# Three blocks a turn in the networks without weights to broadcast, six banks and twelve buffers

## The chip, the core and the metric

The kernel runs on one core of one Trainium2 chip. The metric is the device time of one execution in microseconds (us). Before the change it is 3207.71 us, the median of three runs (3206.38 to 3210.78).

## What is computed

The reference is a small vision tower: 64 sequences of 129 tokens with 64 channels each, kept as h (a tokenizer in front makes them from images). Eight stages follow, each added to h after a layer norm: attention and a network, four times over, of different kinds. What matters here are the networks:

```python
# L0_ffn: 8 experts, hidden width 128, the two best of a gate's scores taken
h = gelu(einsum('td,edh->teh', x, W1) + b1)
y = einsum('teh,ehd->ted', h, W2) + b2
out = einsum('ted,te->td', y, mask)          # mask is 1 for two experts, else 0

# L1_attn: four layers, each with linear attention and then
x = x + gelu(ln(x) @ W1[l] + bf1[l]) @ W2[l] + bf2[l]     # 64 -> 256 -> 64

# L1_ffn: half of each sequence's tokens, times a router weight, 64 -> 256 -> 64
# L3_ffn: 8 experts of width 256 with a capacity, relu, times the gate's probability
```

## The kernel before

All tokens lie in SBUF as one array of 128 partitions by 4128 columns: partitions 0 to 63 are the channels of the first 32 sequences, 64 to 127 those of the other 32 (the two halves, HALVES = 2). Columns are worked in 12 tiles of 344 (TILE, TILES). The stages are phases one behind the other; a phase is a Block, at whose end all engines meet, and the next phase starts when the last one has come.

The function mlp_phase (L642) is one such phase. It serves seven networks: L0's experts (L3894), the four dense networks of L1 (L2570, one a layer), L1's half network (L2713) and L3's experts (L2914). In the last two the result is multiplied by a weight for each token. The weights are spread over the partitions by a matmul of its own (WeightedAddTo.broadcast, L2604) into one of two auxiliary banks, aux_ps, which ScalarE copies out. The other five calls end in AddTo (L845), whose broadcast is None: there nothing writes or reads aux_ps.

The hidden width is cut into blocks of 128: 8 blocks (one for each expert) in L0, 2 in a layer of L1. A step is one block of one tile, so a phase has 12 x blocks steps: 96 in L0, 24 in a layer of L1. For each step and half:

- TensorE raises (raise_hidden, L690): w_up, 64 rows by 128 columns, times the tile's half, into a bank of hid_ps. The two halves sit in different rows of the array. In L0 a second matmul in bf16 (L696) adds -1e30 to the tokens that the expert isn't chosen for. A bank must have been emptied by ScalarE (wait on act_done, k - ring + 1).
- ScalarE (L743) takes the bank through GELU with the bias into a buffer of hid.
- TensorE lowers (lower, L716): w_down, 128 rows by 64 columns, times the buffer, added up in the output bank y_ps of the tile; the two halves go to different columns of the array and different partitions of the bank. In L0 each tile ends with a matmul for the experts' bias (L723).
- VectorE adds the tile's output to h or x (L854, L855), once its last block is lowered. In the last layer of L1, GpSimd also adds that to h (L758).

In the trace each fp32 product of TensorE is two matmul instructions (two passes), and the two halves run side by side. The order on TensorE is written out by hand:

```python
for s in range(0, steps + span, span):
    for k in range(s, min(s + span, steps)):
        raise_hidden(k)
    for k in range(max(s - span, 0), min(s, steps)):
        lower(k)
```

A turn of this loop raises span steps and then lowers the span steps of the turn before. With span = 2 that is four products up (two steps, two halves) and four down. The banks are ring = 4 for the hidden values, 2 for the outputs and 2 auxiliary ones, eight in all, which is the whole of PSUM; the buffers of hid are 8. In L3's experts a DMA brings a row for every mask and VectorE multiplies it in (L792); in L0 no DMA runs in the phase.

Of the kernel before, what the change touches and what calls it, by code (L numbers as in the profile page):

```python
# [78 lines left out]
@contextmanager  # L79
def phase(tower):  # L80
    with ExitStack() as stack:
        ph = Phase(tower, stack)
        yield ph
    for s in ph.used:
        s.base += s.total
        tower.free.append(s)
# [554 lines left out]

def mlp_phase(tower, net, func, x, finish, load, experts=None, sum_into=None, store=None):  # L642

    nc, ring, span = tower.nc, 4, 2
    hidden_ring, row_ring = 8, 6
    with phase(tower) as ph:
        w_up, w_down, b_up = net["up"], net["down"], net["bias"]
        w_extra = net["extra"] if experts else None
        blocks = w_up.shape[1]
        hid_ps = [ph.ps(f"hid{r}") for r in range(ring)]  # L650
        y_ps = [ph.ps(f"y{u}") for u in range(2)]
        aux_ps = [ph.ps(f"aux{u}") for u in range(2)]
        hid = [ph.sb(f"hidden{r}", [P, TILE]) for r in range(hidden_ring)]
        steps = TILES * blocks
        up_done = ph.counts(HALVES * steps)
# [1896 lines left out]
def linear_tower(tower, nc, h, x, column):  # L2552

    with ExitStack() as stack:

        hn = stack.enter_context(nc.sbuf_tensor("lin_hn", [P, COLS], F32))
        v_ends = stack.enter_context(nc.sbuf_tensor("lin_v_ends", [TRIO, TRIOS, TRIO, P], F32))
        with ExitStack() as inner:
            pos = inner.enter_context(nc.sbuf_tensor("lin_pos", [P, 4 * SEQ], F32))
            norm_phase(tower, h, x, 1e-5, pos=pos, loads=[(pos, "L1_pos"), (tower.head_blocks, "L1_blocks")])  # L2560
        for l in range(4):
            with ExitStack() as layer:
                maps = Held(layer, tower, f"lin{l}", [(n, [P, P], f"L1_{n}{l}") for n in ("wq", "wk", "wv", "wo")])
                norm_phase(tower, x, hn, 1e-5, gamma=column(f"L1_g1{l}"), beta=column(f"L1_b1{l}"), loads=maps.loads)
                linear_attention_phase(tower, hn, x, maps, column(f"L1_bo{l}"), v_ends, l == 0)
            with ExitStack() as layer:
                net = network(layer, tower, ("L1", l))
                norm_phase(tower, x, hn, 1e-5, gamma=column(f"L1_g2{l}"), beta=column(f"L1_b2{l}"), loads=net.loads,
                           then=ACT.Gelu)
                mlp_phase(tower, net, ACT.Gelu, hn, AddTo(x, column(f"L1_bf2{l}")), None,  # L2570
                          sum_into=h if l == 3 else None)
# [68 lines left out]
def half_ffn(tower, nc, h, x, column):  # L2640

    with ExitStack() as stack:
# [4 lines left out]
        with phase(tower) as ph:  # L2647
# [12 lines left out]
            with nc.Block() as block:  # L2660
# [31 lines left out]
                def _(dve):  # L2692
# [18 lines left out]
                    assert done[0] == 2 * rounds + 3  # L2711
        finish = WeightedAddTo(tower, h, column("L1f_b2"), tower.spread2, rows)
        mlp_phase(tower, net, ACT.Gelu_apprx_tanh, x, finish, finish.load)  # L2713


# [189 lines left out]
def capacity_ffn(tower, nc, h, x, out):  # L2905
    with ExitStack() as stack:
        rows_t = stack.enter_context(nc.sbuf_tensor("cap_rows", [P, COLS], F32))
        marks16 = stack.enter_context(nc.sbuf_tensor("cap_marks16", [P, COLS], BF16))
        net, gate = network(stack, tower, ("L3", ""), "L3_down_b"), gate_weights(stack, tower, "L3")
        counts = Held(stack, tower, "capacity", [("counting", [P, 2, P], "L3_counting"), ("spread", [P, P], "L3_spread")])  # L2910
        gated_norm_phase(tower, h, x, 1e-5, gate, rows_t, 1, copy16=marks16, offset=0.0, counting=counts["counting"],
                         loads=net.loads + gate.loads + counts.loads, then=ACT.Relu)
        finish = WeightedAddTo(tower, h, 0.0, counts["spread"], rows_t, finite=True)
        mlp_phase(tower, net, ACT.Relu, x, finish, finish.load, Experts(rows_t, 2, marks16=marks16), store=out)  # L2914
# [1094 lines left out]
```

## Time and profile before

| | |
|---|---|
| median of 3 runs | 3207.71 us |
| profiled execution, its own time | 3208.76 us |
| its span, first to last instruction | 3207.0 us |
| TensorE busy in the span | 3012.3 us (94%) |
| L0's experts, from the first raise to the last read | 573.5 to 723.4 us |
| L1's four dense networks | 847.2 to 880.6, 986.6 to 1020, 1124.6 to 1158, 1262.5 to 1297 us |
| granted TensorE clock over the span | 0.99 |

PE is TensorE, PEld its weight loads, ACT ScalarE, DVE VectorE, POOL GpSimd. Times in a view are microseconds from the start of the span. TensorE's matmuls overlap in the pipeline: a matmul of these networks is recorded with 0.45 us, but another starts while it ends, so a row of several matmuls is shorter than their sum, and TensorE can be called busy all through a stretch in which it streams no data for a part of the time.

### The profile page before, as it was taken

What the parts mean: (1) busy time and instruction counts of PE and PEld (TensorE: products, weight loads), DVE (VectorE), ACT (ScalarE), POOL (GpSimd) and SP (SyncE); (2) the same over time, 40 slices, a digit from 0 to 9 for tenths busy, and PEclk for the clock granted to TensorE, in tenths of its full rate; (3) what the DMA queues carried; (4) which work ended last, traced back from release to release, by engine and by line L of the source; (5) the groups of instructions that cost most, each with busy time, mean ns of one, the idle gap of its engine ahead of it and who ended that gap; (6) DMA issues with size and microseconds to landing.
All of it is one profiled execution on the core that took longest, in us unless ns stands there. A gap on an engine that the chain in (4) does not pass through costs nothing. (4 is left out here: it accounts for less than half of the span.)

```text
span 3207.0 us, 61051 instructions
## 1 busy us (share of the span) xinstructions
PE 3012.3 (94%) x22529; PEld 1889.7 (59%) x22561; DVE 2147.3 (67%) x4191; ACT 1736.0 (54%) x3881; POOL 1170.7 (37%) x1151
## 2 busy tenths in 40 slices
PE   7999989999999999999899999997899999989999
PEld 6999867446565655467565543334566666664444
DVE  7999835106474645359669744447999999956777
ACT  1322334566667566657535443344666666665666
POOL 4666611001010101018357323225777777740000
PEclk9999989999999999999999999999999999999999
DMA  2000000000000000000000032210000000004776
GB/s 92 16 16 16 1 19 13 1 1 8 3 5 7 4 5 4 4 7 2 9 1 1 28 76 54 58 43 19 17 7 5 5 5 5 4 25 43 68 67 66
DMA packets 75679, 66.43 MB, mean 21 GB/s; under 512 B 20518, under 2 KB 70857, under 8 KB 74969
## 3 DMA queue, kind: packets, MB, share of 16 engines
q1 hardware_dynamic: 75384, 62.52, 11.6%
q8 instruction: 183, 3.00, 0.4%
q14 instruction: 112, 0.91, 0.1%
HBM read 55.58 MB, written 2.51 MB: 18 GB/s over the span
## 5 line engine op out<-in xcount | busy, mean ns | idle before, releaser
L743 ACT ACTIVATE p_hidden<-p_hid_ps,net_bias 128x344 f32<-128x344 f32 x816 | 382.4, 549 | 225.7 <-PE p_hid_ps L690 167.1
L716 PE MATMUL p_y_ps<-p_hidden,net_down 128*64 128x344 f32 x1632 | 286.0, 467 | 4.6 <-DVE p_hidden L792 4.6
L2875 DVE TENSOR_TENSOR p_hid<-p_silu,p_pair_ps 128x344 f32<-128x344 f32 x288 | 134.8, 509 | 161.5 <-PE p_pair_ps L2824 82.5
L690 PE MATMUL p_hid_ps<-xn,net_up 64*128 64x344 f32 x1248 | 238.0, 481 | 1.2 <-PEq L333 0.6
L792 DVE TENSOR_TENSOR p_hidden<-p_hidden,p_row 128x344 f32<-128x344 f32 x384 | 175.1, 514 | 78.8 <-ACT p_hidden L743 44.1
L2856 ACT ACTIVATE p_silu<-p_pair_ps 128x344 f32<-128x344 f32 x288 | 116.0, 454 | 190.8 <-PE p_pair_ps L2813 190.8
L1983 POOL TENSOR_TENSOR p_prob<-p_prob,p_total 128x1024 f32<-128x1024 f32 (+1 forms) x128 | 185.3, 1469 | 52.5 <-DVE p_total L2171 52.5
L2546 POOL TENSOR_TENSOR p_qt<-p_qt,p_q_sum 97x512 f32<-97x512 f32 (+1 forms) x44 | 46.4, 1054 | 427.3 <-DVE p_q_sum L2489 427.3
L716 PEld LDWEIGHTS p_y_ps<-p_hidden,net_down 128*64 128x64 f32 x1632 | 103.3, 136 | 160.6 <-issue 49.7
L1970 POOL TENSOR_TENSOR p_rot<-p_rot,p_cross 128x512 f32<-128x512 f32 x128 | 160.1, 1273 | 96.4 <-DVE p_cross L2145 96.4
L2802 POOL TENSOR_TENSOR p_weighted<-routed_hn,sent_row 128x344 f32<-128x344 f32 x96 | 89.1, 950 | 241.3 <-PE p_pair_ps L2829 206.3
L690 PEld LDWEIGHTS p_hid_ps<-xn,net_up 64*128 64x128 f32 x1248 | 104.5, 186 | 121.0 <-ACT p_hidden L743 77.4
L1205 POOL TENSOR_TENSOR p_prob<-p_prob,p_total 128x516 f32<-128x516 f32 (+1 forms) x128 | 130.8, 1043 | 66.7 <-DVE p_total L1327 66.7
L154 PE MATMUL p_var_ps<-p_square,average 128*128 128x344 f32 x360 | 139.1, 470 | 2.4 <-DVE p_square L204 1.3
L1824 PE MATMUL p_late_ps<-shared_keys,p_q_t 64*128 64x128 f32 x1024 | 136.7, 287 | 0.0
L1824 PE MATMUL p_early_ps<-shared_keys,p_q_t 64*128 64x64 f32 x1024 | 129.4, 267 | 0.0
L1824 PEld LDWEIGHTS p_early_ps<-shared_keys,p_q_t 64*128 64x128 f32 x1024 | 126.7, 191 | 0.0
L2168 DVE TENSOR_REDUCE p_total<-p_prob 128x8 f32<-128x1024 f32 (+1 forms) x128 | 115.7, 945 | 16.4 <-ACT p_prob L2044 16.4
L3034 PE MATMUL p_c_ps<-p_in,p_crossed 128*128 128x128 f32 (+1 forms) x768 | 126.0, 286 | 0.0
L1824 PEld LDWEIGHTS p_late_ps<-shared_keys,p_q_t 64*128 64x128 f32 x1024 | 124.3, 189 | 0.0
L1977 POOL TENSOR_TENSOR p_rot<-p_rot,p_root 128x1024 f32<-128x1024 f32 x64 | 121.8, 1903 | 0.2
L2037 ACT ACTIVATE p_q_t<-p_t_ps 128x512 f32<-128x512 f32 x128 | 75.9, 594 | 81.3 <-PE p_t_ps L1799 81.3
(487 smaller groups left out, 8045.9 us busy)
## 6 DMA issues: line engine op xcount, KB each, us to landing
sent_row<-gated_rows SPq DMA_DIRECT2D x192, 86.0 KB, 2.9
p_row<-mark_rows SPq DMA_DIRECT2D x192, 86.0 KB, 10.3
tok_x<-in_tok_x SPq DMA_DIRECT2D x11, 384.0 KB, 3.1
out<-h SPq DMA_DIRECT2D x12, 172.0 KB, 3.6
shared_swapped<-xn SPq DMA_DIRECT2D x64, 32.0 KB, 1.9
shared_value_pairs<-shared_values SPq DMA_DIRECT2D x16, 128.0 KB, 2.5
p_x<-in_tok_x SPq DMA_DIRECT2D x5, 384.0 KB, 3.1
p_kinds<-in_tok_c3w SPq DMA_DIRECT2D x1, 1280.0 KB, 7.2
```

Source lines behind the costliest of these rows:

```text
L154: pe.matmul(var_ps[t % var_banks][:, 0:TILE], tower.average[:], square[t % ring][:], start=True, stop=True).then_inc(var_ready.sem, 1)
L690: mm = pe.matmul(hid_ps[k % ring][:, 0:TILE], w_up[half(g), n, :], x[half(g), cols(t)], start=True, stop=not experts or by_rows)
L716: mm = pe.matmul(y_ps[u][half(g), 0:TILE], w_down[:, n, :], hid[k % hidden_ring][:], start=n == 0, stop=last and not experts)
L743: act.activation(hid[k % hidden_ring][:], hid_ps[k % ring][:, 0:TILE], func, bias=b_up[:, n:n + 1]).then_inc(act_done.sem, 1)
L792: dve.tensor_tensor(hid[k % hidden_ring][:], hid[k % hidden_ring][:], row[x % row_ring][:, g, :], ALU.mult).then_inc(masked.sem, 1)
L1205: pool.tensor_tensor(p[:], p[:], total[(j - 1) % 2][:, g, :, None] .to_broadcast([P, HEADS, seen]), ALU.mult).then_inc(scaled.sem, 1)
L1824: return pe.matmul(ps[:, c * wide:(c + 1) * wide], q, keys_t[half(p), b, 0:wide], start=ty == LATE and i == 0, stop=ty == EARLY and i == 3)
L1970: pool.tensor_tensor(a[:, :, s, :], a[:, :, s, :], x[:, :, 1 - s, :], ALU.add).then_inc(added.sem, 1)
L1977: pool.tensor_tensor(r, r, root[n % ring_q][:, :, None].to_broadcast([P, Q_HEADS, D]), ALU.mult).then_inc(normed.sem, 1)
L1983: pool.tensor_tensor(p[:], p[:], total[n % 2][:, ty, :, None].to_broadcast([P, MS, wide]), ALU.mult).then_inc(scaled.sem, 1)
L2875: dve.tensor_tensor(hid[n % ring_h][g][:], silu[n % 2][g][:], c_of(n, g)[:, 0:TILE], ALU.mult).then_inc(hid_ready.sem, 1)
L3034: pe.matmul(sides[:, :, side, :].rearrange("p n (b i) -> p n b i", i=half_rows), weights, shifted(group, y, s), start=False, stop=closes[0 ...
```

## The change

In a call whose finish has no broadcast, a turn raises three steps and lowers three, the hidden banks are six and the hidden buffers twelve. The two auxiliary banks are not allocated there. In a call with a broadcast everything stays: four banks, span 2, eight buffers.

```diff
 def mlp_phase(tower, net, func, x, finish, load, experts=None, sum_into=None, store=None):
 
-    nc, ring, span = tower.nc, 4, 2
-    hidden_ring, row_ring = 8, 6
+    nc = tower.nc
+    ring, span = (4, 2) if finish.broadcast else (6, 3)
+    hidden_ring, row_ring = 2 * ring, 6
...
-        aux_ps = [ph.ps(f"aux{u}") for u in range(2)]
+        aux_ps = [ph.ps(f"aux{u}") for u in range(2)] if finish.broadcast else None
```

## Rows read from the trace of the kernel before

**Rows 1.** The page's first part: engine, busy us, share, instructions.
```profile
PE 3012.3 (94%) x22529; PEld 1889.7 (59%) x22561; DVE 2147.3 (67%) x4191; ACT 1736.0 (54%) x3881; POOL 1170.7 (37%) x1151
```

**Rows 2.** Busy time by stretch: L0, one layer of L1, half network, L3's experts.
```profile
core 0: us, PE busy (x) PEld busy (x) DVE busy (x) ACT busy (x) POOL busy (x), PEclk, DMA share, GB/s
573.50:723.50 150.00, 149.31 (x1008) 67.81 (x1008) 6.20 (x12) 90.71 (x193) 0.00 (x0) 1.00 0.00 1
847.20:880.60 33.40, 32.70 (x192) 14.73 (x192) 6.92 (x12) 23.53 (x49) 0.00 (x0) 1.00 0.00 1
...
1335.00:1378.00 43.00, 42.67 (x214) 16.68 (x216) 11.33 (x21) 28.05 (x61) 0.00 (x0) 1.00 0.00 1
2914.00:3199.00 285.00, 280.36 (x1596) 122.08 (x1596) 206.51 (x482) 184.13 (x396) 0.00 (x0) 0.99 0.71 68
```

**Rows 3.** Waits in 847 to 880: who waited for whom, us, times, longest.
```profile
DVE xn L855 <- PE p_y_ps L716: 26.2, 11, 5.4
ACT p_hidden L743 <- PE p_hid_ps L690: 9.6, 11, 1.3
PEld p_hid_ps L690 <- ACT p_hidden L743: 5.9, 11, 0.6
```

**Rows 4.** TensorE in order of time, 862 to 868 (L1): start, duration, what.
```profile
862.73 1.43 PE L690 MATMUL p_hid_ps<-lin_hn,net_up 64*128 64x344 f32 x8
864.09 1.38 PE L716 MATMUL p_y_ps<-p_hidden,net_down 128*64 128x344 f32 x8
865.39 1.43 PE L690 MATMUL p_hid_ps<-lin_hn,net_up 64*128 64x344 f32 x8
```

**Rows 5.** ScalarE in order of time, 847 to 868 (L1).
```profile
848.07 3.62 ACT L743 ACTIVATE p_hidden<-p_hid_ps,net_bias 128x344 f32<-128x344 f32 x8 [1.15 <-PE p_hid_ps L690]
...
863.61 1.86 ACT L743 ACTIVATE p_hidden<-p_hid_ps,net_bias 128x344 f32<-128x344 f32 x4 [0.80 <-PE p_hid_ps L690]
```

**Rows 6.** TensorE in order of time, first and last turns of a layer of L1.
```profile
847.22 3.61 PE L690 MATMUL p_hid_ps<-lin_hn,net_up 64*128 64x344 f32 x16 [0.40 <-PEq L134]
850.76 1.38 PE L716 MATMUL p_y_ps<-p_hidden,net_down 128*64 128x344 f32 x8
...
876.05 1.43 PE L690 MATMUL p_hid_ps<-lin_hn,net_up 64*128 64x344 f32 x8
877.41 2.53 PE L716 MATMUL p_y_ps<-p_hidden,net_down 128*64 128x344 f32 x16
```

**Rows 7.** TensorE's weight loads in order of time, 862 to 868 (L1).
```profile
862.73 0.88 PEld L690 LDWEIGHTS p_hid_ps<-lin_hn,net_up 64*128 64x128 f32 x8 [0.53 <-ACT p_hidden L743]
864.09 0.78 PEld L716 LDWEIGHTS p_y_ps<-p_hidden,net_down 128*64 128x64 f32 x8 [0.48 <-issue]
```

**Rows 8.** TensorE in order of time, 640 to 643 (a turn of L0).
```profile
640.70 0.85 PE L690 MATMUL p_hid_ps<-xn,net_up 64*128 64x344 f32 x4
641.38 0.31 PE L696 MATMUL p_hid_ps<-unmarked,banish 64*128 64x344 bf16 x2
641.53 0.74 PE L690 MATMUL p_hid_ps<-xn,net_up 64*128 64x344 f32 x4
642.11 0.31 PE L696 MATMUL p_hid_ps<-unmarked,banish 64*128 64x344 bf16 x2
642.35 1.38 PE L716 MATMUL p_y_ps<-p_hidden,net_down 128*64 128x344 f32 x8
```

**Rows 9.** TensorE in order of time, L0's first and last lowerings.
```profile
577.37 1.38 PE L716 MATMUL p_y_ps<-p_hidden,net_down 128*64 128x344 f32 x8
...
719.74 2.53 PE L716 MATMUL p_y_ps<-p_hidden,net_down 128*64 128x344 f32 x16
722.10 0.75 PE L723 MATMUL p_y_ps<-marks,net_extra 128*64 128x344 f32 x4
```

**Rows 10.** VectorE (layer one) and GpSimd (layer four) at the network's end.
```profile
880.02 0.58 DVE L855 SCALAR_TENSOR_TENSOR xn<-p_y_ps,columns,xn 128x344 f32<-128x344 f32 x1 [0.58 <-PE p_y_ps L716]
...
1296.03 0.91 POOL L758 TENSOR_TENSOR h<-h,xn 128x344 f32<-128x344 f32 x1 [0.25 <-DVE xn L855]
```

**Rows 11.** Busy time by stretch, columns as in group 2, behind two attentions.
```profile
828.00:833.00 5.00, 4.88 (x11) 3.02 (x12) 0.14 (x1) 2.13 (x5) 0.00 (x0) 0.66 0.16 40
1104.00:1109.00 5.00, 3.35 (x11) 1.49 (x10) 1.11 (x2) 1.09 (x3) 0.00 (x0) 1.00 0.16 39
```

## The prediction

> **What bounds the kernel now.** I read the page's sums first, to see which engine is full, then the stretches of the five networks that the change touches, then, inside one of them, who waits for whom, and last the order in time of the single turns.
>
> TensorE is busy for 94% of the span [rows 1]. Five networks have no weights to broadcast: L0's experts and the four dense networks of L1. In L0's stretch TensorE is busy 149.31 of 150.00 us, in a layer of L1 32.70 of 33.40, both at the full granted clock of 1.00, that is 2.4 GHz; ScalarE has 90.71 and 23.53 [rows 2]. The two networks whose results are weighted (L1's half network, L3's experts; 43 and 285 us, [rows 2]) keep their loops, so the change has 150 + 4 x 33.4 = 284 us to work on. ScalarE and VectorE wait for TensorE in L1's stretch (9.6 and 26.2 us), and TensorE's weight loads show idle time "until ScalarE" [rows 3].
>
> That last entry would suggest that TensorE lacks free banks. It doesn't: in a steady turn of L1 the raises start at 862.73 and again at 865.39 [rows 4], while ScalarE's four GELUs start at 863.61 and take 1.86 us, so end at 865.47, with 0.80 us of idle time before them in every turn [rows 5]. Their ends lie (1.86 - 0.55) / 3 = 0.44 apart, so the first bank is free at 864.16, 1.2 us before it is wanted again, and the fourth at 865.47, while its raise comes at least three pairs (0.87 us, below) after 865.39, at 866.3. TensorE sets the pace, with its own stream.
>
> The stream has a seam. A turn of L1 is 2.665 us (850.76 to 877.41 is ten turns, [rows 6]). The work in it is 8 pairs of matmuls: each product goes in two passes, and the two halves of the batch run side by side. One pair costs (2.53 - 1.38) / 4 = 0.288 us, from 16 lowering matmuls in a row against 8 [rows 4, 6]. 8 x 0.288 = 2.30, so 0.36 us of each turn is no streaming. It lies at the two seams: from the raises' start to the lowerings' start is 1.36 us for 4 pairs (1.15), and from there to the next raises 1.30. The weight loads show it: they stop for 0.53 us ahead of the raises and 0.48 us ahead of the lowerings [rows 7]. Within a run of one kind there is no such hole: in L0 the second block's four raising matmuls start 641.53 and its masks 642.11, 0.58 for two pairs, although that block waits for banks as the first does [rows 8].
>
> **The change, part by part.** In these five networks a turn raises three blocks and lowers three in place of two and two. No matmul, GELU, addition or DMA is added or removed; the two auxiliary banks that nobody read there become hidden banks five and six, and the hidden buffers go from 8 to 12.
>
> Term 1, the steady turn. The third block brings its pure work and no seam. In L1 that is 4 pairs, 4 x 0.288 = 1.15, so the turn becomes 2.665 + 1.15 = 3.82 us for six products. In L0 a block also has its mask pass: 0.15 us (641.38 to 641.53), so 1.30 us; the turn goes from 2.957 to 4.26. The 2.957 is (719.74 - 577.37 - 11 x 0.577) / 46: 46 turns, and 11 tile ends with four matmuls for the experts' bias, two pairs each [rows 8, 9]. 24 blocks make 8 turns in place of 12, 96 blocks 32 in place of 48, and two fewer than that lie between the first and the last-but-one lowering: 6 in place of 10, 30 in place of 46.
>
> Term 2, the ramp. At the start two turns of raises run before anything is lowered. Today four products go through at once and four wait for ScalarE, whose step is (3.62 - 0.56) / 7 = 0.437 us [rows 5]; the first lowering starts at 850.76. Then six go at once, six wait, and the last of these waits for the sixth GELU, not the fourth: 2 x 0.44 = 0.88 us later, at 851.64, but with 12 products raised in place of 8. In L0 likewise 577.37 becomes 578.25.
>
> Term 3, the tail. The last two turns are lowered in a row: today 8 pairs, 2.53 us, then 12, 2.53 + 1.15 = 3.68. ScalarE doesn't delay it: its last GELU ends about 0.88 (862.73 to 863.61) + 5 x 0.437 + 0.55 = 3.6 us after the last raises began, and the last lowering turn starts at about 3.7, its sixth product 1.5 us later. The table load behind it (L752) has more room than before.
>
> L1, per layer: before, 877.41 + 2.53 = 879.94. After, 851.64 + 6 x 3.82 + 3.68 = 878.24. Gain 1.7 us; four layers 6.8.
> L0: before, 719.74 + 2.53 = 722.27 and the last bias. After, 578.25 + 30 x 4.26 + 11 x 0.577 + 3.68 = 716.1, and the same bias. Gain 6.2 us.
> Sum: 13.0 us.
>
> Costed at nothing. The output bank: a tile now often ends in the middle of a turn, and block 0 of tile t waits for the reading of tile t - 2. That tile's last block is three blocks earlier in L1, so the wait falls within a run of lowerings in the last two turns alone. There it has 1 + 4 pairs, 1.44 us, from the last pair's start, and the reading ends 0.45 (the pair) + 0.08 + 0.58 = 1.11 after it [rows 10]: hidden by 0.3 us; without that cover it would cost at most 0.6 us once a layer. POOL's sum in the last layer takes 0.91 us a tile, less than the 1.15 between two tiles' ends, and its last sits behind the end as now [rows 10]. The buffers: ScalarE writes a buffer that was lowered one turn earlier, now as before. All phases behind simply start earlier.
>
> These networks lie on the path: phases are divided by a barrier, and what follows waits for the last read. So 13.0 us comes off the profiled execution's 3208.76 us (span 3207.0), which is 1.05 us above the median of the three runs, 3207.71: 3194.7 us.
>
> Bounds of the unknown, a third block in a run: at best it costs its pure work (above), at worst the turn grows in proportion, by 1.33 us in L1 and 1.48 in L0, as if each block carried its share of the hole. I take the first, since [rows 8] show a second block without a hole, and the second for the range.
>
> **The rivals.** (a) The hole belongs to the blocks or their waits, not to the seam. Then 850.76 + 0.88 + 6 x 4.00 + 3.68 = 879.3 (0.6 us less) in L1 and 578.25 + 30 x 4.44 + 6.35 + 3.68 = 721.5 (0.8 us less) in L0: 3 us in all, 3204.5, inside what I call no change. For it: the hole's length is charged to ScalarE in the waits, and the raises do carry semaphores. Against it: the mask rows and the sixteen lowerings in a row. The Trainium skill's page "TensorE: Matmul & The Clock Gate", in "The mechanism", says that weight loads are pulled ahead of running matmuls in a 64-deep window where the row groups don't conflict; by that, a change of kind would leave no hole and fewer changes would win nothing but ramp and tail. The page "TensorEngine Tiling (Array Packing)", in "Key Properties", says that a change of tiling mode drains the engine, and raises (64 rows x 128 columns) and lowerings (128 x 64) are two modes. The holes of 0.53 and 0.48 us in the loads side with the second.
>
> (b) Slower: ScalarE becomes the bound. All six banks are filled and emptied once a turn, so a turn can't be shorter than six GELU steps: 6 x 0.44 = 2.6 us against 3.82 (L1) and 4.26 (L0). It would decide from a step of 0.64 us, and end above today's time from 4.00 / 6 = 0.67 in L1. At 0.75: 4.50 a turn, 6 x 0.50 x 4 = 12 us lost in L1 and 2 in L0, less the 3 of ramp and tail: 3219. For it: PSUM is full, with no bank aside. Against it: the step is 0.43 to 0.44 in both networks, and ScalarE's slack before each turn grows.
>
> (c) The clock gives some back, or adds. Behind L1's attention the granted clock falls in two layers of four: 0.66 over 5 us at 828, but 1.00 at the same place at 1104, with 11 matmuls and 5 of ScalarE's instructions in the one, 11 and 3 in the other [rows 11]. A fall costs 0.34 x 5 = 1.7 us. Whether it comes may depend on the moment, and that moves when all behind L0 comes 6 us earlier: these four sites alone give 3.4 us either way, 3191.3 to 3198.1, and there are others. It would need eight more falls to eat the gain.
>
> **How the numbers follow.** Forecast as summed, clock within a fall or two: 0.74. (c) at 3 us or more either way: 0.12. (a), whole or half (3199.6 to 3204.5): 0.11. (b): 0.03. The range reaches from the forecast less 5 us (clock) to 7 above it, into half of (a): 3190 to 3202. What a measurement can tell from no change is 0.2%, 6.4 us. Faster: 0.87; same, from (a): 0.10; slower: 0.03.
>
> **What would show it.** In the order in time of L1: raises x12, lowerings x12, period 3.82 us, and 4.26 in L0; the x12 lowerings last 1.38 + 0.58 = 1.96 us. A period of 4.0 in L1 is (a); idle time of ScalarE going to nothing is (b). First lowering 4.42 us after the first raise (3.54 now); last run x24, 3.68 us. L0's network ends 6.2 us sooner, each L1 network is 1.7 shorter; L1's half network and L3's experts keep their lengths. The prediction is wrong if these hold and the total doesn't move, or if the gain comes from elsewhere.

## The result and the profile after

The changed kernel takes 3199.64 us (median of 9 runs, 3189.67 to 3202.47), the kernel before 3209.12 (9 runs, 3206.38 to 3213.99): a ratio of 0.9966, 95% interval 0.9957 to 0.9975. Two more measurements on other occasions gave 0.9961 (0.9947 to 0.9974) and 0.9948 (0.9931 to 0.9966). The forecast was 13.0 us less, a ratio of 0.9959, which lies in all three intervals. It is faster; by the first measurement by 9.5 us, by the other two by 12 and 17. The time forecast, 3194.7 us, was 4.9 us too low: 3.5 us of that is gain that didn't come in this measurement, 1.4 us the base, since the nine runs of the kernel before have their median at 3209.12 and not at 3207.71.

The profiled execution took 3199.91 us, its span is 3198.0 us, 9.0 less than before. The stretches of the same networks, as in [rows 2], come out of the trace of the changed kernel so (stretch, us, busy us of TensorE, its loads, VectorE, ScalarE, GpSimd, granted clock, DMA):

```profile
572.90:716.90 144.00, 143.11 (x1008) 69.81 (x1008) 6.20 (x12) 88.85 (x193) 0.00 (x0) 1.00 0.00 1
838.90:871.00 32.10, 31.04 (x192) 15.67 (x192) 6.91 (x12) 23.09 (x49) 0.00 (x0) 1.00 0.00 1
1320.40:1363.50 43.10, 43.07 (x216) 16.76 (x216) 11.69 (x22) 28.44 (x61) 0.00 (x0) 1.00 0.00 0
2905.00:3190.00 285.00, 279.77 (x1592) 122.30 (x1593) 207.03 (x482) 183.99 (x396) 0.00 (x0) 0.99 0.70 68
```

L0's network needs 144 us where it needed 150, L1's 32 where it needed 33.4 to 33.7, with the same 1008 and 192 matmuls. TensorE is busy all through, as before: the busy share hides what changed. From barrier to barrier the phases are 150.18 and 143.99 us in L0 (6.19 less), 33.69 and 32.01 in L1 (1.68 less, in each of the four): 12.9 us in all. Of the other two calls of the function, L1's half network is unchanged (44.9 us); L3's experts were forecast to keep their length and took 0.7 us longer, 293.2 us before and 293.9 after, from the first raise to the end of the span.

TensorE in order of time in L1, the steady turns, answers to [rows 4]:

```profile
852.97 2.01 PE L691 MATMUL p_hid_ps<-lin_hn,net_up 64*128 64x344 f32 x12
854.91 1.96 PE L717 MATMUL p_y_ps<-p_hidden,net_down 128*64 128x344 f32 x12
856.79 2.01 PE L691 MATMUL p_hid_ps<-lin_hn,net_up 64*128 64x344 f32 x12
```

A turn is 856.79 - 852.97 = 3.82 us for six products, 0.637 each, where it was 2.665 for four, 0.666 each. Its weight loads have the same two holes as in [rows 7], once for twelve loads and not for eight:

```profile
852.97 1.46 PEld L691 LDWEIGHTS p_hid_ps<-lin_hn,net_up 64*128 64x128 f32 x12 [0.53 <-ACT p_hidden L744]
854.91 1.35 PEld L717 LDWEIGHTS p_y_ps<-p_hidden,net_down 128*64 128x64 f32 x12 [0.48 <-ACT p_hidden L744]
856.79 1.46 PEld L691 LDWEIGHTS p_hid_ps<-lin_hn,net_up 64*128 64x128 f32 x12 [0.53 <-ACT p_hidden L744]
858.73 1.35 PEld L717 LDWEIGHTS p_y_ps<-p_hidden,net_down 128*64 128x64 f32 x12 [0.48 <-issue]
```

The reader should see how little the name behind the arrow says: the same hole of 0.48 us is charged to ScalarE in one turn and to nobody in the next.

Ramp and tail of that layer, beside [rows 6]:

```profile
839.03 4.49 PE L691 MATMUL p_hid_ps<-lin_hn,net_up 64*128 64x344 f32 x24 [0.40 <-PEq L134]
843.44 0.80 PE L717 MATMUL p_y_ps<-p_hidden,net_down 128*64 128x344 f32 x4
...
864.44 2.01 PE L691 MATMUL p_hid_ps<-lin_hn,net_up 64*128 64x344 f32 x12
866.37 3.69 PE L717 MATMUL p_y_ps<-p_hidden,net_down 128*64 128x344 f32 x24
```

The first lowering comes 4.41 us after the first raise (3.54 before, 4.42 forecast), the last 24 lowering matmuls take 3.69 us (3.68 forecast).

A turn of L0, beside [rows 8]:

```profile
700.34 0.85 PE L691 MATMUL p_hid_ps<-xn,net_up 64*128 64x344 f32 x4
701.02 0.31 PE L697 MATMUL p_hid_ps<-unmarked,banish 64*128 64x344 bf16 x2
...
702.72 1.96 PE L717 MATMUL p_y_ps<-p_hidden,net_down 128*64 128x344 f32 x12
704.60 0.85 PE L691 MATMUL p_hid_ps<-xn,net_up 64*128 64x344 f32 x4
```

704.60 - 700.34 = 4.26 us, as forecast.

What isn't in the forecast is the difference between the networks' 12.9 us and the span's 9.0. It lies in phases that the change doesn't touch. The norms behind L1's four attentions, which [rows 11] looked into: 19.09, 19.09, 17.67 and 17.67 us before, 17.66, 17.67, 19.10 and 17.66 after. Each long one has a granted clock of 0.91 in place of 1.00 (first two lines before, last two after):

```profile
828.10:847.20 19.10, 18.61 (x59) 10.90 (x61) 10.60 (x24) 15.97 (x37) 0.00 (x0) 0.91 0.04 11
1106.90:1124.60 17.70, 17.20 (x59) 9.99 (x61) 10.60 (x24) 15.94 (x37) 0.00 (x0) 1.00 0.05 12
```
```profile
821.30:839.00 17.70, 17.25 (x60) 9.96 (x61) 10.60 (x24) 15.94 (x37) 0.00 (x0) 1.00 0.04 12
1093.90:1113.00 19.10, 18.69 (x60) 10.94 (x60) 10.60 (x24) 15.94 (x37) 0.00 (x0) 0.91 0.04 11
```

One fewer of these gives 1.4 us. L3's attention takes back more, in its front part (55.06 to 57.55 us) and its main part (652.35 to 656.15). Before, then after:

```profile
2159.20:2214.20 55.00, 43.99 (x284) 27.05 (x288) 39.83 (x64) 33.25 (x76) 28.49 (x26) 0.94 0.09 28
```
```profile
2144.40:2201.90 57.50, 47.55 (x281) 29.64 (x282) 39.01 (x63) 32.37 (x75) 28.58 (x26) 0.85 0.09 27
```

At 0.94 over 55.0 us the clock was short by 3.3 us, at 0.85 over 57.5 by 8.6; in the main part it was 1.00 before and 0.99 after. Together the two parts took 6.3 us longer. Their instructions are the same, and the clock is what differs, so I put the loss down to it; no edit shows that, but the lengths and clocks of all fourteen traces go together (below, at the end of the experiments).

The account of the span: 12.9 us from the five networks, 1.4 from the norm, 0.6 ahead of L0's experts and 1.1 between L3's attention and its experts are won, 6.3 in the two parts of the attention and 0.7 in L3's experts are lost, which leaves 9.0.

### The profile page after: what moved, and what is told of

It is laid out like the page before. It is cut to its first block and busy times, and to the rows that moved or that the text cites. A ratio compares the mean times of both kernels' runs of the same rounds, so it can differ in the third digit from the quotient of the medians.

```text
span 3198.0 us, 61063 instructions
## 1 busy us (share of the span) xinstructions
PE 3007.4 (94%) x22561; PEld 1899.4 (59%) x22561; DVE 2148.3 (67%) x4191; ACT 1732.2 (54%) x3881; POOL 1170.7 (37%) x1151
```

## The experiments

The theory under test: in these networks TensorE pays a fixed seam of some 0.36 us each time it goes from raising to lowering and back, since the two use the array in different shapes; the change wins by having fewer turns. The rival: TensorE lacked banks, or the hole belongs to each block and its waits.

**Banks alone.** Six banks, twelve buffers, but two blocks a turn.

```diff
-    ring, span = (4, 2) if finish.broadcast else (6, 3)
+    ring, span = (4, 2) if finish.broadcast else (6, 2)
```

> Six hidden banks and twelve buffers as in the changed kernel, but still two blocks raised and two lowered a turn. Theory (the gain is the seam between raising and lowering, paid once a turn): the steady turn stays 2.665 us in L1 and 2.957 us in L0; only the ramp shortens, since the last product of the second turn then waits for the second GELU and not the fourth, 2 x 0.44 us. Each of the five networks 0.9 us shorter, 4.4 us in all. Rival (TensorE lacked free banks, as the waits that are charged to ScalarE suggest): the turns shorten by themselves, L0's network by some 6 us and a layer of L1 by 1.7 us, as in the changed kernel.

Measured: 3205.16 us, one run (before, beside it, 3214.35). L0's phase 149.45 us, 0.73 less; L1's 32.82, 0.87 less. The steady turn is as it was (lines of its trace in L1):

```profile
864.03 1.43 PE L691 MATMUL p_hid_ps<-lin_hn,net_up 64*128 64x344 f32 x8
865.38 1.38 PE L717 MATMUL p_y_ps<-p_hidden,net_down 128*64 128x344 f32 x8
866.69 1.43 PE L691 MATMUL p_hid_ps<-lin_hn,net_up 64*128 64x344 f32 x8
```

866.69 - 864.03 = 2.66. More banks without larger turns shorten the ramp and nothing else: in L1 the first lowering comes 2.66 us after the first raise, where it was 3.54, in L0 3.10 where it was 3.83.

**One block a turn.**

```diff
-    nc, ring, span = tower.nc, 4, 2
+    nc, ring = tower.nc, 4
+    span = 2 if finish.broadcast else 1
```

> The kernel before, but one block raised and one lowered a turn in the five networks (four banks, eight buffers). Theory: a seam costs 0.36 us whatever the turn holds, so a turn is 4 x 0.288 + 0.36 = 1.51 us in L1 and 1.66 in L0, and there are twice as many. L1: the ramp shortens by about 0.9 us with two products less raised in it, some 3.5 us longer in a layer (33.7 to about 37.2); L0 some 16 us longer (150.2 to about 166). Rival (the hole belongs to the blocks or their waits): the lengths stay within 1 us of before.

Measured: 3243.84 us, one run. L0 167.25 us (17.1 more), L1 37.93 (4.2 more). The turn of L1:

```profile
871.25 0.85 PE L691 MATMUL p_hid_ps<-lin_hn,net_up 64*128 64x344 f32 x4
872.03 0.80 PE L717 MATMUL p_y_ps<-p_hidden,net_down 128*64 128x344 f32 x4
872.76 0.85 PE L691 MATMUL p_hid_ps<-lin_hn,net_up 64*128 64x344 f32 x4
```

1.51 us for one block, where turns of two and three took 2.665 and 3.82: equal steps of 1.155, and a rest of 0.355 at none. That line through three points is the seam. The networks grew by some 1 us more than I expected. In L1 this lies at the two ends of the phase: the first four lowering matmuls take 1.23 us and the last eight 1.93, where without a wait for ScalarE they would take 0.80 and 1.38.

**A foreign shape, or a foreign matmul.** Two kernels put a tiny matmul between the two raised blocks of a turn, into an auxiliary bank; it waits for nothing. In the first it uses 128 rows x 64 columns of the array, as the lowerings do:

```diff
                     for k in range(s, min(s + span, steps)):
                         raise_hidden(k)
+                        if not finish.broadcast and k == s:
+                            pe.matmul(aux_ps[0][0:D, 0:32], tower.ones[:, 0:D], tower.banish[:, 0, 0:32], start=True, stop=True)
```

> The kernel before with one tiny bf16 matmul (128 rows x 64 columns of the array, 32 moving columns, into an auxiliary bank that nobody reads) between the two raised blocks of each turn, in the five networks. It waits for nothing. Theory (the hole is the change of the array's tiling): it adds two more changes, about 0.36 us a turn: L1's turn 2.665 to about 3.05, a layer about 4 us longer; L0's turn 2.957 to about 3.3, about 17 us longer. Rival (the hole comes from waiting on semaphores at the head of a run, or belongs to each block): the tiny matmul costs no more than its own issue, under 0.1 us a turn.

In the second 64 rows x 128 columns, as the raises:

```diff
+                            pe.matmul(aux_ps[0][:, 0:32], tower.ones[0:D, :], tower.banish[0:D, 0, 0:32], start=True, stop=True)
```

> The same tiny matmul at the same place, but on 64 rows x 128 columns of the array, as the raises around it, so that the tiling isn't changed. Theory: under 0.1 us a turn, L1's turn at most 2.76 us and L0's at most 3.06. Rival (any foreign matmul in the run costs a hole): as with the other shape, 0.36 us a turn.

Measured, one run each: 3234.58 and 3219.24 us. L0 165.76 and 155.01, L1 37.10 and 34.74 (150.18 and 33.69 before). First the foreign shape, then the same shape, in L1:

```profile
864.50 0.85 PE L690 MATMUL p_hid_ps<-lin_hn,net_up 64*128 64x344 f32 x4
865.28 0.20 PE L732 MATMUL p_aux_ps<-banish,ones 128*64 128x32 bf16 x1
865.41 0.85 PE L690 MATMUL p_hid_ps<-lin_hn,net_up 64*128 64x344 f32 x4
866.19 1.38 PE L716 MATMUL p_y_ps<-p_hidden,net_down 128*64 128x344 f32 x8
867.50 0.85 PE L690 MATMUL p_hid_ps<-lin_hn,net_up 64*128 64x344 f32 x4
```
```profile
862.70 0.85 PE L690 MATMUL p_hid_ps<-lin_hn,net_up 64*128 64x344 f32 x4
863.38 0.18 PE L732 MATMUL p_aux_ps<-banish,ones 64*128 64x32 bf16 x1
863.39 0.84 PE L690 MATMUL p_hid_ps<-lin_hn,net_up 64*128 64x344 f32 x4
864.16 1.38 PE L716 MATMUL p_y_ps<-p_hidden,net_down 128*64 128x344 f32 x8
865.47 0.85 PE L690 MATMUL p_hid_ps<-lin_hn,net_up 64*128 64x344 f32 x4
```

The turn grows from 2.665 to 3.00 us with the foreign shape (0.34) and to 2.77 with the same (0.10: the four raises behind it take 0.84 us, where the second four in [rows 8] take 0.74). A hole needs no wait and no block of its own, only another shape of the array. The size is known less sharply: if the tiny matmul itself costs in the foreign shape what it costs in the same, the two changes of shape alone are 0.24 us, otherwise up to 0.34, and the seam of a turn is 0.36. Nor do these runs tell the change of shape from the fact that a matmul on all 128 rows needs the rows of both halves. The first expectation was nearly met (0.34 for 0.36; a layer 3.4 us longer for 4), the second came out just beyond its edge of 0.1.

**Three blocks on four banks.** The turn without the banks.

```diff
-    ring, span = (4, 2) if finish.broadcast else (6, 3)
-    hidden_ring, row_ring = 2 * ring, 6
+    ring, span = (4, 2) if finish.broadcast else (4, 3)
+    hidden_ring, row_ring = 4 * span, 6
```

> Three blocks raised and three lowered a turn, but on the four banks of before (12 buffers). Theory: the fifth and sixth raise of a turn wait for the first two GELUs of the same turn, which end 1.4 and 1.9 us after its start in L1; that costs more than the seam gives. L1's networks 35 to 37.5 us (33.7 before), L0's 152 to 160 us (150.2 before). Rival (fewer seams are worth having with any number of banks): L1 at 32.5 or less, L0 at 145 or less.

Measured: 3240.37 us, one run. L1 37.42 us, at the upper end; L0 163.33, 3 us beyond it. In L1 the twelve raising matmuls of a turn take 2.76 us where with six banks they take 2.01:

```profile
867.06 2.76 PE L691 MATMUL p_hid_ps<-lin_hn,net_up 64*128 64x344 f32 x12
```

The larger turn alone is a loss of 3.7 us a layer, the banks alone a gain of 0.9, both together a gain of 1.7: the larger turn needs the banks.

**Four blocks a turn on six banks.**

```diff
-    ring, span = (4, 2) if finish.broadcast else (6, 3)
-    hidden_ring, row_ring = 2 * ring, 6
+    ring, span = (4, 2) if finish.broadcast else (6, 4)
+    hidden_ring, row_ring = 4 * span, 6
```

> Four blocks raised and four lowered a turn on six banks (16 buffers) in the five networks. Theory (a longer run of raises pays until its products catch up with ScalarE, which frees a bank every 0.44 us where a raise takes 0.29 us in L1 and 0.36 in L0; from there the two halves no longer run side by side): in L0 the eighth product of a turn is ready for its bank in time, so the turn is 2.957 + 2 x 1.298 = 5.55 us and the network about 141.3 us, 2.7 less than with three. In L1 the eighth product comes at 1.83 us, 0.1 before its bank is free, and its block is raised one half behind the other: about 0.3 us a turn lost, the network at 32.5 to 33.2 us, longer than the 32.0 with three. Rival (only the number of seams counts): both networks get shorter, L1's to 31.9 or less.

Measured: 3192.76 us, one run (before 3213.09). L0 141.47 us, 2.5 less than with three; L1 32.60, 0.6 more. Both as expected, in opposite directions. The sixteen raises of L1 take 2.76 us, where sixteen side by side would take 2.01 + 0.58 = 2.59, and the turn 5.15:

```profile
853.08 2.76 PE L691 MATMUL p_hid_ps<-lin_hn,net_up 64*128 64x344 f32 x16
855.77 2.53 PE L717 MATMUL p_y_ps<-p_hidden,net_down 128*64 128x344 f32 x16
858.23 2.76 PE L691 MATMUL p_hid_ps<-lin_hn,net_up 64*128 64x344 f32 x16
```

5.15 for eight products is 0.644 each, more than 0.637 with six; the longer ramp comes on top. The fourth block's second half starts at 854.99, when ScalarE has given up its bank (854.95), 0.08 us behind the first half; the run of raises comes out 0.17 us longer. The wait in one half costs about twice its length.

**Turns of unequal size, up to seven.** In mlp_phase a list of turns takes the place of the fixed span.

```diff
+    groups = [2, 4, 6] + [7] * 12 if experts else [2, 3, 5, 5, 5, 4]
+    hidden_ring = 4 * max(groups) if groups else 2 * ring
...
+                    at = [sum(groups[:i]) for i in range(len(groups) + 1)]
+                    for i in range(len(groups) + 1):
+                        for k in range(at[i], at[min(i + 1, len(groups))]):
+                            raise_hidden(k)
+                        for k in range(at[max(i - 1, 0)], at[i]):
+                            lower(k)
```

> Six banks as in the changed kernel, but turns of unequal size in the five networks: L0 raises 2, 4, 6 and then twelve times 7 blocks (28 buffers), a layer of L1 2, 3, 5, 5, 5, 4 blocks (20 buffers). Theory (a seam costs 0.36 us whatever stands in the turn, and the ramp is shorter with a small first turn): L0 has 15 turns in place of 32 and is some 5.5 us shorter than in the changed kernel (144.0 to about 138.5), a layer of L1 some 0.7 us (32.0 to about 31.3); 8 us in all, before what the later stages' clock takes or gives (3 us to either side). Rival (with more than six products in a row TensorE waits for ScalarE's banks and loses what the seams give): L0's network stays at 142 us or more, L1's at 32.

Measured: 3196.32 us (5 runs, ratio to before 0.9956, 0.9944 to 0.9969), beside the changed kernel's 3197.71. L0 142.32 us, 1.7 less than in the changed kernel and not 5.5; L1 32.61, 0.6 more and not 0.7 less. My expectation was wrong and the rival half right. The turn's end in L0 shows why:

```profile
639.62 0.94 PE L695 MATMUL p_hid_ps<-xn,net_up 64*128 64x344 f32 x4
640.20 0.31 PE L701 MATMUL p_hid_ps<-unmarked,banish 64*128 64x344 bf16 x1
640.35 0.45 PE L695 MATMUL p_hid_ps<-xn,net_up 64*128 64x344 f32 x1
640.40 0.31 PE L701 MATMUL p_hid_ps<-unmarked,banish 64*128 64x344 bf16 x1
```

The masks, which elsewhere come as x2, come singly: the two halves are out of step. In the next turn, which starts at 645.71, the second half of the sixth block starts at 649.53, 0.09 us behind the first, when ScalarE has given up its bank (649.49), and that of the seventh at 650.41, 0.25 us behind, for a bank given up at 650.36. The lowerings start at 651.33, where seven blocks side by side would let them start at 650.98: 0.35 us lost in a turn, which the two waits nearly make up, and about 4 us in twelve turns. The expectation had counted no wait at all.

**Turns of five in L0, three in L1.** The same list, with [2, 4] + [5] * 18 and [3] * 8.

> L0's network in turns of 2, 4 and then eighteen times 5 blocks on six banks (20 buffers); L1's stay in turns of three as in the changed kernel. Theory: five blocks are the most that L0 can raise before it has to wait for a bank within the turn, so 20 turns in place of 32 take 12 x 0.36 = 4.3 us off: L0's network 144.0 to about 139.7 us, the four of L1 stay 32.0 us. The total is 4 us under the changed kernel's, up to 3 us more or less by the later stages' clock. Rival (runs of more than six products lose it again, as in the kernel with turns of seven): L0 stays above 142 us.

Measured: 3191.92 us (6 runs, 3188.35 to 3194.27), ratio to before 0.9934 (0.9915 to 0.9953). L0 140.40 us, 0.7 above the expected 139.7, L1 32.00. The last block's masks of a turn take 0.35 us and not 0.31, so five is already at the edge (18 x 0.04 = 0.7 us). Six blocks a turn throughout were not run. Beside it ran the changed kernel:

> The changed kernel itself, beside the one with turns of five and the kernel before. The networks 144.0 and 32.0 us, as in both looks so far; the total 9 to 13 us under the kernel before, the spread between its runs coming from the stretches at half clock.

3196.15 us (6 runs, 3193.11 to 3200.45), 0.9948 (0.9931 to 0.9966), 17 us under a kernel before that ran at 3213.09 on that occasion (11 runs, 3204.09 to 3219.05). The expected 9 to 13 us were missed; the changed kernel's own time was within 2 us of its time in e5_again, and the kernel before was 3 us slower. The turns of five beat it by 4.2 us, which is close to the 3.6 us of their shorter phase; the two intervals against before overlap.

**Where the rest went.** The changed kernel again, measured together with the next two:

> The changed kernel itself, on the same chip as the next three. The five networks should be shorter than before by 6.2 us (L0) and 1.7 us (each of L1), 12.9 us in all. Theory (part of it is given back in later stages, because TensorE's half-clock stretches fall otherwise when these stages run earlier): the total gains 9 to 10 us. Rival (the 9.5 us of the first measurement were an accident of its runs): the total gains the full 13 us.

3197.71 us (5 runs, 3196.32 to 3198.04) against 3209.76 (15 runs): 12.05 less. All five networks' phases agree with the first profile to 0.02 us. Neither the 9.5 nor the 13 is refuted.

Then idle matmuls behind L1's fourth network shift all that follows:

```diff
+                if sum_into is not None:
+                    pe.wait_ge(act_done.sem, act_done.at(HALVES * steps))
+                    for _ in range(75):
+                        pe.matmul(hid_ps[0][:], tower.ones[:], tower.banish[:, 0:4, :], start=True, stop=True)
```

> The changed kernel with 75 idle matmuls (bf16, 512 columns, some 0.216 us each) behind the last lowering of L1's fourth network, so that everything after it starts about 15 us later than in the changed kernel, where it did before the change. Theory (what is given back depends on when the later stages run): these stages lose less time at the half clock, as before the change, and the total grows by 15 less 3 to 4 us, to within 2 us of the kernel before. Rival (what is lost later doesn't depend on the moment): the total grows by the full 15 us, to 5 to 6 us above the kernel before.

The phase grew by 14.6 us, the total by 13.4, to 3211.09 (11 runs; ratio to before 1.0002, 0.9993 to 1.0011). That is between the two and tells them apart badly. Its trace goes against the moment as the cause in L3's attention: the front part starts within 1.1 us of where it did in the kernel before, yet takes 57.54 us at a clock of 0.85, as in the changed kernel:

```profile
2158.70:2216.30 57.60, 47.09 (x281) 29.62 (x284) 39.62 (x64) 32.80 (x75) 28.56 (x26) 0.85 0.09 27
```

With 40 in place of 75:

> The same with 40 idle matmuls, about 7.5 us. Theory: the later stages' loss at the half clock takes yet another value; the total differs from the changed kernel's by something other than 7.5 us, by more than 1.5 us to either side, and the stretches at 0.5 in the profile account for the difference. Rival: the total grows by 7.5 us.

7.1 us were put in and the total grew by 3.9, to 3201.56 (5 runs, 3195.39 to 3201.66). In the profile L3's main part took 653.11 us, not 656.15, and the granted clock over the span is 0.987 against 0.984. Between this profile and the one with 75, which run the same instructions in L3's attention, that stage differs by 3 us.

**All traces side by side.** Nothing that was edited lies in the last two stages, so the fourteen traces can be compared there. From the start of L3's attention to the first raise of its experts:

| length, us | clock short by, us | traces |
|---|---|---|
| 754.6 | 10.2 | before, e10_three_on_four |
| 756.0 to 757.1 | 13.7 | e2_span1, e7_shift7, e9_span4, e11_fives |
| 758.2 to 758.8 | 17.1 | e1_banks_only, e3_tiny_other, e4_tiny_same, e8_graded, e12_again |
| 759.6 to 759.8 | 18.8 | after, e5_again, e6_shift15 |

The second column is (1 - granted clock) x length. The length follows it, about 0.6 us for each us that the clock is short, and doesn't follow the moment: the stage starts at 2159 us in the kernel before and at 2189 in e10_three_on_four, at 2155 in e1_banks_only and at 2196 in e2_span1.

L3's experts vary more, from 288.8 to 295.5 us, and there the clock is not what goes with it. The changed kernel twice, e5_again and then e12_again, from the first raise to the end, each with columns as in [rows 2] and its line of waits as in [rows 3]:

```profile
2904.20:3194.50 290.30, 280.30 (x1608) 122.83 (x1608) 211.01 (x492) 184.29 (x396) 0.00 (x0) 0.99 0.69 67
DVE p_hidden L793 <- DMA p_row<-mark_rows: 25.4, 19, 9.2
2903.10:3198.60 295.50, 283.75 (x1608) 123.47 (x1608) 210.70 (x492) 183.95 (x396) 0.00 (x0) 0.98 0.68 66
DVE p_hidden L793 <- DMA p_row<-mark_rows: 35.5, 26, 9.2
```

VectorE waits 10 us more for the mask rows that a DMA brings, and the stage takes 5.2 us more. Over the fourteen traces this wait is 20 to 25 us in the three shortest of these stages (288.8 to 289.8 us), 25 to 33 in the next six (290.3 to 292.2) and 33 to 38 in the five longest (293.2 to 295.5). Why the rows come later in one execution than in another isn't shown.

## Why the prediction was right

The forecast of 13.0 us less held in its mechanism and nearly in its terms.

- Term 1, the steady turn: 3.82 and 4.26 us forecast, 3.82 and 4.26 measured. The choice between the bounds, that a third block brings only its pure work, was right; spans one, two and three lie on one line.
- Term 2, the ramp: 0.88 us later forecast, 0.87 in L1, 0.88 in L0. The kernel with banks alone shows the same step of two GELUs with the other sign: with six banks and turns of two, lowering starts 0.88 us earlier in L1 than on four banks.
- Term 3, the tail: 3.68 forecast, 3.69 measured.
- Their sum: 6.2 and 1.7 us a network forecast, 6.19 and 1.68 measured; 13.0 and 12.9 in all.
- Costed at nothing, the tile that ends within a turn: the last lowering run of L1 is one piece of 24 matmuls, without a hole.
- Rival (a), the hole belongs to blocks or their waits: false, by the turn's length and by the tiny matmul of another shape. The Trainium skill's "TensorEngine Tiling (Array Packing)", "Key Properties", has the rule that bears here (a change of mode drains the engine): the 0.34 us for the foreign shape, against 0.10 for the same, agree with it, and the page gives no price. The prediction set against it the pull-ahead of weight loads, which the Trainium skill's "TensorE: Matmul & The Clock Gate", "The mechanism", states for row groups that don't conflict. A lowering takes all 128 rows and so conflicts with every raise, and that rule alone never promised that there would be no hole; in these traces the loads stop for 0.53 and 0.48 us at each change.
- Rival (b), ScalarE as the bound: it doesn't bind at three blocks (1.08 us of idle time before each turn's GELUs in L1, 0.80 before the change). In a form that I had not seen it sets the limit, through the banks: at four in L1, and in L0 with a first 0.04 us a turn at five.
- Rival (c), the clock: the place was right, since two norms got their clock back and one lost it. But the larger share, 6.3 us in L3's attention in the profiled pair, came where I had named no place. A fall was also priced too high: 1.7 us is what the clock was short by in such a norm, and the norm took 1.43 longer. The total fell short of 13 by 3.5 us in the first measurement, 1 in the second, and went beyond by 4 in the third. That the rest stayed at 3.9 us in the profiled pair is in part luck: stages that the forecast held constant won 3.1 us and lost 7.0, and L3's experts, which it took to keep their length, differ by 5.2 us between two profiles of the same kernel.

What stays open: which executions lose clock in L3's attention, and which wait longer for the mask rows in L3's experts. The same kernel took 656.15 and 655.10 us in the attention's main part in two profiles, 57.55 and 57.54 in the front part, and 1 us less over both in a third; the kernel before had 652.35 and 55.06 in its one profile. Whether running earlier makes that loss likelier isn't shown. That it depends on the moment alone doesn't hold at 15 us; the 7 us run only shows that the total need not grow by what was put in.

## What to carry to other kernels

Where TensorE alternates between two shapes of the array, count the changes of shape: here each round trip cost 0.36 us that no busy share showed, and grouping more products of one shape between them is worth it until the group outruns the engine that frees the banks. Enlarge the group and the banks together, up to the product that would first wait within its own turn, and take that point for each network from its own times: of the sizes run, three blocks were best in L1 and five in L0. A wait in one of two halves that run side by side can cost more than its length: 0.17 us for 0.08 in L1 with four blocks. And before a difference of a few microseconds is put down to a change, compare the stages that the change doesn't touch: here they alone moved by up to 7 us from trace to trace.

## What the runs showed of the hardware that was not expected

- Raised side by side, a product costs 0.29 us of TensorE's time. Where one half waits for its bank the halves fall out of step: 0.08 us of waiting in L1 with four blocks made the run of raises 0.17 us longer. Where every raise waits, as in the ramp, they follow each other by 0.44 us, which is ScalarE's step.
- A matmul of 32 columns between two runs of the same shape, in one half of the array only, added 0.10 us a turn; in another shape 0.34.
- The norms behind L1's attentions have two lengths in all fourteen traces, 17.66 and 19.09 us, within 0.05 us, and nothing between, at granted clocks of 1.00 and 0.91.
- The same stage with the same instructions took 754.6 us where the clock was short by 10.2 us in it and 759.8 where by 18.8.
